# One core of Trainium2: the experts' last product with tokens on the output's partitions, and a new slot table

## What is computed

```python
h = _L0_tok_ref(x, ...)          # three layer norms and 5-wide convolutions, a fourth norm, res @ out_w + out_b: (64, 128, 64)
h = h + _L0_attn_ref(_layernorm(h), ...)   # 8 heads, logits -sum_w |q[s,h,w] - k[t,h,w]| / 8, softmax, values twice (a and a transposed)
h = h + _L0_ffn_ref(_layernorm(h), ...)

# _L0_ffn_ref: 32 experts, one per token
logits = xf @ router_w.T + router_b
idx = jnp.argmax(logits, axis=-1)
h = relu(einsum('nd,ndh->nh', xf, W1[idx]) + b1[idx])      # hidden size 16
out = relu(einsum('nh,nhd->nd', h, W2[idx]) + b2[idx])
```

## Time and profile before

| | us |
|---|---|
| median of 3 runs | 3468.23 (3464.18 to 3468.46) |
| the profiled execution | 3481.97 |
| its span, first to last instruction | 3480.2 |
| VectorE busy | 3130.7 (90%) |
| TensorE matmuls busy | 3227.9 (93%) |
| GpSimd busy | 2849.9 (82%) |
| ScalarE busy | 2577.4 (74%) |

### The profile page before, as it was taken

One profiled execution on the slowest core, in us unless ns is written; L12 is line 12 of the kernel. 1 busy time (PEld: TensorE's weight loads), 2 busy tenths in 40 slices (PEclk: granted clock), 3 DMA queues, 4 the chain that ended last, 5 costly groups with the idle time before them and its releaser, 6 DMA issues. The chain is left out here.

```text
span 3480.2 us, 78005 instructions
## 1 busy us (share of the span) xinstructions
PE 3227.9 (93%) x23116; PEld 2461.7 (71%) x23116; DVE 3130.7 (90%) x4358; ACT 2577.4 (74%) x4378; POOL 2849.9 (82%) x2728
## 2 busy tenths in 40 slices
PE   8899999999999999999999999999999999999888
PEld 6677777776777777777777777767777777777655
DVE  5899999999999999999999999999999999999876
ACT  3777787777777777777777777777777777777763
POOL 3788888888888888888888888888888888888874
PEclk9999999999999999999999999999999999999988
DMA  6778777778777778777777777787777787777773
GB/s 136 152 156 161 154 158 158 153 154 166 155 152 158 153 153 166 156 156 153 156 157 158 157 157 154 154 165 153 157 158 153 155 163 157 155 155 153 157 152 70
DMA packets 199652, 534.96 MB, mean 154 GB/s; under 512 B 69142, under 2 KB 133398, under 8 KB 150968
## 3 DMA queue, kind: packets, MB, share of 16 engines
q0 software_dynamic: 73728, 492.86, 71.4%
q1 hardware_dynamic: 125880, 41.54, 5.9%
HBM read 10.93 MB, written 2.10 MB: 4 GB/s over the span
## 5 line engine op out<-in xcount | busy, mean ns | idle before, releaser
L925 DVE TENSOR_REDUCE S<-psU 128x16 f32<-128x1024 f32 x2216 | 2629.9, 1217 | 235.4 <-PE psU L487 220.9
L487 PE MATMUL psU<-flat,kT 99*128 99x256 bf16 x16384 | 2291.6, 275 | 189.9 <-DVE S L925 119.4
L712 ACT ACTIVATE absd<-psU 128x1024 f32<-128x1024 f32 x1880 | 1913.4, 1023 | 587.0 <-PE psU L487 575.9
L487 PEld LDWEIGHTS psU<-flat,kT 99*128 99x128 bf16 x16384 | 1498.0, 98 | 832.1 <-DVE S L925 316.8
L1183 POOL TENSOR_TENSOR absd<-absd 128x1024 f32<-128x1024 f32 (+2 forms) x512 | 1183.5, 2312 | 111.3 <-DMA absd<-absd 110.1
L1189 POOL TENSOR_TENSOR absd<-absd 128x512 f32<-128x512 f32 (+4 forms) x768 | 767.5, 999 | 60.2
L1171 POOL DMA_DIRECT2D absd<-absd x512 | 454.0, 887 | 244.8 <-ACT absd L712 186.2
L499 PE MATMUL psC<-c1in,w 128*128 128x384 f32 (+1 forms) x930 | 314.3, 421 | 17.0 <-DVE c1in L969 16.9
L591 PE MATMUL psZ<-P,v 128*128 128x256 f32 x1024 | 279.1, 379 | 0.0
L936 DVE TENSOR_REDUCE S<-absd 128x64 f32<-128x512 f32 (+4 forms) x512 | 264.3, 516 | 1.3 <-POOL absd L1189 1.3
L518 PE MATMUL psC<-c3in,w 128*128 128x128 f32 x1240 | 245.8, 282 | 1.7 <-DVE c3in L969 1.7
(11 more groups left out here) (180 smaller groups left out, 2266.8 us busy)
## 6 DMA issues: line engine op xcount, KB each, us to landing
absd<-absd POOLq DMA_DIRECT2D x379, 1024.0 KB, 8.1
absd<-absd POOLq DMA_DIRECT2D x98, 768.0 KB, 6.5
flat<-qparts SPq DMA_DIRECT2D x3072, 8.0 KB, 4.0
absd<-absd POOLq DMA_DIRECT2D x35, 512.0 KB, 4.6
xin<-in_x SPq DMA_DIRECT2D x32, 192.0 KB, 6.4
flat<-pattern SPq DMA_DIRECT2D x4, 768.0 KB, 10.9
out_h<-result SPq DMA_DIRECT2D x32, 64.0 KB, 6.1
w<-in_w SPq DMA_DIRECT2D x1, 1280.0 KB
```

Source lines behind the costliest of these rows:

```text
L487: mm = nc.tensor.matmul(psU[:, slot % PLACES, m], kT[0:ROWS + 3, b, m, :], flat[0:ROWS + 3, half % HALVES, :, lo:lo + BLOCK], start=True, ...
L712: nc.scalar.activation(absd[:, c % GROUPS, :, u], psU[:, slot % PLACES].rearrange("p (n a) s w -> p n (a s w)", n=2), ACT.Abs).then_inc(a_ ...
L925: nc.vector.tensor_reduce(S[:, b, hd, SB * c:SB * c + SB], psU[:, slot % PLACES].rearrange("p a s w -> p s a w"), AX.XY, ALU.add, apply_ab ...
```

## The change

The output product swaps its operands: hT (for the bias: the one-hot ohT) becomes the stationary block, one sample's 128 tokens at a time, and the weights with 64 columns the moving one. The result then has the tokens on its partitions, as h2 has. So there are ten matmuls of 64 columns instead of five of 256, the relus into fT and the transpose back go, and VectorE takes relu and addition in one `scalar_tensor_tensor`. The weights are held and loaded once. In the tables turnb goes from slot 45 to 48, route from 74 to 75, out is spread over 7 slots instead of 4, stat goes from 1 to 5, and the lists for the lead-in, the last pair and the idle matmuls are new. VectorE's result stays in slot 101.

```diff
--- before
+++ after
@@ -62,7 +62,7 @@
-SHARED_LAST = {8: (0, 2, 4, 6), 9: (0, 2), 10: (0, 1), 11: (0, 2), 12: (0, 3, 6), 13: (2, 4, 6), 14: (0, 2, 4), 15: (0, 3)}
+SHARED_LAST = {8: (0, 2), 9: (1, 3), 10: (0, 4), 11: (2, 6), 12: (0, 4), 13: (1, 5), 14: (0, 2, 4), 15: (0, 3)}
@@ -109,10 +109,10 @@
-EX_PE = Steps("fan turn route turnoh hida hidb out back")
+EX_PE = Steps("fan turn route turnoh hida hidb out")
 EX_DVE = Steps("h2 stat0 stat1 wait aggr0 aggr1 max rev0 rev1 max2 noh result")
 EX_POOL = Steps("var rstd mean shift")
-EX_ACT = Steps("x0 x1 turned0 turned noh oh relua relub relu0 relu")
+EX_ACT = Steps("x0 x1 turned0 turned noh oh relua relub")
@@ -126,23 +126,23 @@
-AT1 = dict(vf=3, vb=5, v_len=0, turn_len=0, exp=25, exp_len=4, rden=38, scale=33, scale_len=19, turna=43, turnb=45,
+AT1 = dict(vf=3, vb=5, v_len=0, turn_len=0, exp=25, exp_len=4, rden=38, scale=33, scale_len=19, turna=43, turnb=48,
            pv=51, pv_len=3, half=52, sum=54, tanh=55, gate=60)
 AT_AT = (AT0, AT1)
 SECOND = 66
-EX_AT = dict(fan=62, h2=62, rstd=61, x=65, turn=67, route=74, pick=76, turnoh=82, hida=87, hidb=89, hid_len=0, out=92,
-             out_len=4, back=100)
-NORM_AT = dict(stat=1, rstd=2, x=9, turn=24, part1=20, rest1=19, part2=50, part3=50, hx=82)
+EX_AT = dict(fan=62, h2=62, rstd=61, x=65, turn=67, route=75, pick=76, turnoh=82, hida=87, hidb=89, hid_len=0, out=92,
+             out_len=7, result=101)
+NORM_AT = dict(stat=5, rstd=2, x=9, turn=24, part1=20, rest1=19, part2=50, part3=50, hx=82)
 HAND_AT = dict(xT=12, hx=83)
 TOK_AT = dict(copy=3, a=7, conv1=14, len1=22, b=47, conv2=56, len2=10, c=67, conv3=76, len3=33, d=112, turn=121,
               out=126, root=0, gap=4)
-LEAD_IN = [(36, 18), (41, 21), (52, 22), (56, 24), (59, 24), (66, 29), (71, 37), (77, 37), (79, 39), (81, 41),
-           (81, 56), (117, 68), (118, 75), (128, 78)]
-LEAD_LAST = (92, 111, 124)
-LEAD_TAIL = 0
-WEIGH = (2, 3)
+LEAD_IN = [(21, 11), (40, 16), (42, 16), (44, 24), (54, 24), (54, 24), (66, 27), (66, 27), (66, 28), (66, 28),
+           (75, 54), (117, 68), (128, 82)]
+LEAD_LAST = (90, 111, 117)
+LEAD_TAIL = 4
+WEIGH = (4, 5)
@@ -181,7 +181,7 @@
-STILL = dict(turna=18, fan=0, turn=21, route=9, turnoh=13, hida=7)
+STILL = dict(turna=20, fan=2, turn=26, route=4, turnoh=8, hida=6)
@@ -239,8 +239,8 @@
-        we2 = sb("we2", [T, 4, 2, LAT])
-        be2 = sb("be2", [T, 2, LAT])
+        we2 = sb("we2", [T, 4, LAT])
+        be2 = sb("be2", [T, LAT])
@@ -299,7 +299,6 @@
-        fT = sb("fT", [T, T])
@@ -347,12 +346,12 @@
-            (w3[:], a["w3"]), (b3[:], a["b3"]), (ln1g_col[:], a["ln1g_col"]), (ln1b_col[:], a["ln1b_col"]), (wout[:], a["wout"]),
-            (bout[:], a["bout"]), (rank[:], a["rank"]), (we2[:, :, 0, :], a["we2"]), (we2[:, :, 1, :], a["we2"]),
+            (w3, a["w3"]), (b3, a["b3"]), (ln1g_col, a["ln1g_col"]), (ln1b_col, a["ln1b_col"]), (wout, a["wout"]),
+            (bout, a["bout"]), (rank, a["rank"]), (we2, a["we2"]),
         ]
         parts_of = [
             (wqv[0:65, :], a["wqv"]), (wfan[0:65, :], a["wfan"]), (wroute[0:65, :], a["wroute"]),
-            (we1[0:65, :], a["we1"]), (we1[96:128, :], a["shut"]), (be2[0:E, 0, :], a["be2"]), (be2[0:E, 1, :], a["be2"]),
+            (we1[0:65, :], a["we1"]), (we1[96:128, :], a["shut"]), (be2[0:E, :], a["be2"]),
@@ -403,7 +402,7 @@
-                    sp.dma_start(dst, src).then_inc(loaded, 16)
+                    sp.dma_start(dst[:], src).then_inc(loaded, 16)
@@ -628,19 +627,17 @@
-                for q in spread(slot, EX_AT["out"], EX_AT["out_len"], 5):
-                    if q == 0:
-                        take_bank(ex_act, EX_ACT.after(p, "relu"))
-                    if q == 2 and other is not None:
+                for n in spread(slot, EX_AT["out"], EX_AT["out_len"], 10):
+                    b, q = n // 5, n % 5
+                    if n == 0:
+                        take_bank(ex_dve, EX_DVE.after(p, "result"))
+                    if n == 2 and other is not None:
                         pe.wait_ge(ex_act, EX_ACT.after(p, "relub"))
-                    mm = nc.tensor.matmul(psZ[:, 0:256], (be2[:, :, :] if q == 4 else we2[:, q, :, :]).rearrange("p a w -> p (a w)"),
-                                          ohT[:, :] if q == 4 else hT[:, q, :], start=(q == 0), stop=(q == 4))
-                    if q == 4:
+                    mm = nc.tensor.matmul(psZ[:, b * LAT:b * LAT + LAT],
+                                          ohT[:, b * T:b * T + T] if q == 4 else hT[:, q, b * T:b * T + T],
+                                          be2[:, :] if q == 4 else we2[:, q, :], start=(q == 0), stop=(q == 4))
+                    if n == 9:
                         mm.then_inc(ex_pe, 1)
-                if slot == EX_AT["back"]:
-
-                    take_bank(ex_dve, EX_DVE.after(p, "result"))
-                    nc.tensor.transpose(psZ[:, 0:2 * LAT], fT[:, :], ident[:, :]).then_inc(ex_pe, 1)
@@ -868,11 +865,6 @@
-                if slot == EX_AT["out"] + EX_AT["out_len"]:
-                    act.wait_ge(ex_pe, EX_PE.after(p, "out"))
-                    for b in range(2):
-                        nc.scalar.activation(fT[b * LAT:b * LAT + LAT, :], psZ[b * LAT:b * LAT + LAT, b * T:b * T + T],
-                                             ACT.Relu).then_inc(ex_act, 1)
@@ -1057,11 +1049,11 @@
-                if slot == EX_AT["back"] + 1:
-                    dve.wait_ge(ex_pe, EX_PE.after(p, "back"))
+                if slot == EX_AT["result"]:
+                    dve.wait_ge(ex_pe, EX_PE.after(p, "out"))
                     if not (isinstance(p, int) and p == 0):
                         dve.wait_ge(stored, 16 * p)
-                    nc.vector.tensor_tensor(result[:, :, :], zl, h2[:, :, :], ALU.add).then_inc(ex_dve, 1)
+                    nc.vector.scalar_tensor_tensor(result[:, :, :], zl, 0.0, h2[:, :, :], ALU.max, ALU.add).then_inc(ex_dve, 1)
@@ -1116,8 +1108,8 @@
-                        nc.vector.memset(be2[32:64, :, :], 0.0).then_inc(ones, 1)
-                        nc.vector.memset(be2[64:128, :, :], 0.0).then_inc(ones, 1)
+                        nc.vector.memset(be2[32:64, :], 0.0).then_inc(ones, 1)
+                        nc.vector.memset(be2[64:128, :], 0.0).then_inc(ones, 1)
                         for t in (x1T, x1T_late):
                             nc.vector.memset(t[64:65, :], 1.0).then_inc(ones, 1)
                         nc.vector.memset(gT[64:65, :, :], 2.0).then_inc(ones, 1)
```

## The result

The changed kernel takes 3479.85 us, the median of 20 runs (3471.79 to 3490.97), against 3468.39 us for 20 runs of the kernel before (3463.84 to 3479.25): ratio 1.0028, 95% interval 1.0019 to 1.0036. It is slower by about 10 us, where 4.9 us less was forecast, and it lies 1.9 us above the range of 3446 to 3478.

A forecast was written before the change was run, and what follows sets the result against it. VectorE taken as most loaded, only its waits for TensorE units winnable. Steady pairs -2.8, lead-in -1.5, last pair +0.3, tail -0.9 sum to -4.9 us, from 3468.23 to 3463.3 us; range 3446 to 3478.

The forecast's parts named there:

- The output product: Slots 92 to 98: VectorE's waits shrink, but ScalarE closes the stretch and gives the gain back; -0.06 us a pair.
- turnb: Slot 45 to 48: transposes go where TensorE waits for ScalarE; -0.03 us a pair, +0.1 if the copy comes late.
- stat: Norm's statistics, slot 1 to 5: GpSimd held no longer than now, 0; +0.3 us if they came 1 us late.
- What bounds the kernel: VectorE is most loaded; only its idle time waiting for TensorE units, 7 us a pair, can be won.
- Rival (2): Slots 97 and 98: two late matmuls delay unit 98 and VectorE waits; +14.6 us, 3478 us; chance 0.14.
- Rival (1): Output product's stretch: ScalarE isn't its end and the hole is really won; 15.5 us, 3448 us; chance 0.22.
- Rival (3): TensorE's waits for flat: transfers move by half, 17 us, to 3446 or 3480 us; chance 0.08 faster, 0.03 slower.
- Rival (4): Slots do nothing and only the kernel's ends act: 3466 us; chance 0.53 together with the main forecast.
- The passes: Output product on TensorE: twenty passes of 64 moving columns at 0.105 us each, 2.1 us against 2.2 before.
- Lead-in: Start of the kernel: unit 0 starts near 55.2 us; -1.5 us, from -3 to 0.
- Last pair and tail: SHARED_LAST gives VectorE four more units, +0.3 us (-2 to +3); chain after the last product loses relu and transpose, -0.9.
- The base: Whole kernel: profiled execution lies 13.7 us above the runs' median 3468.23; the same 4.9 us is taken from that median.

The follow-up runs named there:

- c4: Kernel before with the swapped product, turnb at 48, route at 75 and out over 7 slots, all else as before: 3474.13 us, ratio 1.0014.
- b2: Changed kernel with turnb, route, out, stat and all lists as before, so the swapped product alone: 3467.79 us, ratio 0.9997 to before.
- c1: Kernel before with one number changed, stat in slot 5 instead of 1: 3477.41 us, ratio 1.0018.
- c3: Changed kernel with stat back in slot 1 and LEAD_TAIL 1 instead of 4: 3474.17 us, ratio 1.0009 to before.
- d3: b2 with the new idle matmul counts and the first sample's eight exponentials laid over slots 93 to 95, out over 4 slots: 3471.30 us, ratio 1.0009 to before.
- d4: d3 with out spread over 7 slots instead of 4: 3455.03 us, ratio 0.9964 to before.
- c2: c1 with the changed kernel's lead-in lists: 3471.49 us, ratio 1.0010 to before.
- b4: Changed kernel with SHARED_LAST, the list for the last pair, as before: 3475.20 us, ratio 1.0026 to before.

## Why the prediction was wrong

**Sum.** Forecast -4.9 us, measured +10 us (0.0028 x 3468). By parts, as ratios give them: the swap with the old slots -1 (0.9997, uncertain by 3); turnb and out +4.3 by the traces, +6 by c4 against b2; stat +6 to +6.6 (each ratio uncertain by 4 to 5); lead-in, last pair and idle matmuls nothing that can be told. -1 + 4.3 + 6.3 = +9.6; with such uncertainties, that it meets the measured 10 so closely is in part luck.

**What bounds the kernel: right, but incomplete.** The sum was judged by VectorE's waits alone. TensorE's own idle time was taken as harmless wherever VectorE lies behind. It isn't: moving it, with VectorE's work unchanged, cost 6 us in c1, and the granted clock fell with it.

**stat, the step that failed most.** GpSimd "holds its next group's DMA and tree, but not longer than now: 0". What was asked there, whether GpSimd comes late, was answered rightly: slots 0 to 16 keep their median of 13.97 us. The mechanism that costs 6 us, the granted clock, was not among the rivals at all. The trace of before had shown it: its clock falls to half for 3.4 us at 389 and at 1761 us, both in slots 12 to 16 of a pair, and a middle stretch with a clock of 1.00 doesn't say that all pairs are like it. That such stretches come more often with stat in slot 5 is shown by c1 and c3. That it is the bunching of TensorE's idle time that brings them is argued from c1 and d3, which bunched it for different reasons; which property of it counts was not measured, and single pairs of before (at 389 and 1761 us) fall with the same waits as their neighbours. The Trainium skill describes such a thing in "TensorE: Matmul & The Clock Gate", section "A second HAM failure mode: psum-queue depth-cycling": short idle times between groups of matmuls that cycle through PSUM make the clock swing between its levels and cost throughput. By that page, which the prediction cited for the weight loads only, this would have been a rival; the runs agree with it in kind, and give it a price here of 0.18% and 0.19% of the time (c1, and c3 against after).

**turnb, the second step that failed.** The waits moved as forecast, and the copy ended as forecast: at 1154.8 in before's time (1156.43 less the 1.64 us by which slot 42 of this pair begins later). What was wrong is that this is "just when pv wants it, behind the unit that is complete at 1155.07". pv doesn't stand behind the end of that unit's row: in the trace of before its first weight load begins at 1154.80 and its first matmul at 1154.91. With units 50 and 51 now 0.08 us earlier, the load could have begun near 1154.7; it begins 0.11 us behind the copy's end, after a wait of 0.19 us. -0.03 was taken; the bound "if the copy comes late, +0.1" is what was measured, and the choice between them was worth 4 us in 31 pairs.

**The output product, right in mechanism, short in size.** VectorE's waits ahead of 91 to 95 fell to 1.30 us (forecast 1.2), TensorE waits for ScalarE ahead of unit 97, and unit 98 comes no earlier. Forecast -0.06 us a pair, measured +0.04 (-0.08 to slot 99, +0.12 behind it; c4 against b2). The reciprocal did go earlier, but unit 98 was complete at 1198.22 in before's time instead of 1198.15, and VectorE, which now waits for it, takes 1.23 us for this reduction, where it took 1.18 directly behind the reciprocal. Rival (2) named this place, and at 1198.22 the kernel came within 0.04 us of its point of decision, 1198.26; its full price of 0.47 us a pair was far too high. Rival (1) did not occur in after, and d4 shows that it was ScalarE that prevented it. Rival (3) did not occur either: the waits for flat are 31.8 us in 33 cases, as before. Rival (4), that only the ends act, 3466 us, is near b2 with 3467.79, whose slots are the old ones.

**The passes.** Six passes of 64 columns take 0.62 us from start to start in b2, 0.103 each, where 0.105 was taken. By the load rule of the Trainium skill ("TensorE: Matmul & The Clock Gate", section "LDWEIGHTS (loading the stationary operand)") it would be an estimated 107 ns for 128 columns, and the trace stands within 4% of it.

**Lead-in.** Unit 0 was forecast near 55.2 us and came at 54.7 (55.5 in c2), so that step worked. -1.5 us was booked for it, and it isn't there at the end of pair 0; c2 can't tell its share from nothing.

**Last pair and tail.** +0.3 was taken for SHARED_LAST; b4 gives 0.0002 between the kernels, no effect that can be measured. From VectorE's last reduction of psU on, nine kernels with the new product take 30.2 to 30.4 us and after 29.4, and the four with the old one 31.0, 31.0, 32.6 and 32.6: the product saves 0.6 us or more there, in agreement with -0.9, and the scatter of 1.6 us allows no closer word. In the two chains it is 0.57 us, where -0.98 + 0.25 - 0.1 = -0.83 was forecast for the same part: the wait and the twenty passes cost 0.41 us more than the ten passes did, not 0.15.

**The base.** 13.7 us between the profiled execution and the median were carried over as a constant. They weren't one: they were for the most part half-clock time at the two ends, and they also put the rows for the last pair in an untypical state.

## What to carry to other kernels

A step moved on an engine can cost time though that engine does the same work, when it moves TensorE's idle time and the granted clock falls more often: look at the granted clock pair by pair, not at the mean of a stretch, and compare the kernels' mean clocks over many runs. When one engine's wait is shortened ahead of a second engine that ends the stretch, neither edit shows alone; the two have to be made together, as d4 shows beside c4 and d3. Where a moved copy lands within 0.1 us of its reader, take the late side, and compare its end with the reader's first weight load, not with the end of the row ahead. Take a second profile before trusting the first one's ends.

## What was new about the hardware

The granted clock of a kernel whose TensorE is busy for 93% of the span falls to half for 3.4 us at a time in the middle of the run, at one place of the loop, and each such stretch costs some 1.4 to 1.5 us (15.45 against 13.98 in c1's pairs; 15.39 against 13.97 in the first profile of before). It happened in 0 to 17 of 27 pairs, by the slots chosen. Within one kernel, too, the timed runs follow it: after's 20 runs go from 3471.8 us at a clock of 0.994 to 3485.2, the mean of the three at 0.986.

A float32 pass with 128 stationary columns and a new stationary block each time takes 0.103 us with 64 moving columns (six in 0.62 us, b2) and 0.22 with 256 (pv in before, six in 1.30 us), so quartering the moving columns only halves it. And a copy that a matmul reads as stationary block has to be there ahead of the matmul's own turn: in before the first weight load of pv begins 0.11 us ahead of its first matmul, and in after it begins 0.11 us behind the end of the copy that it waits for.

VectorE's reduction of 1024 values takes 1.225 us after a wait and 1.216 without one (medians of after's trace), 0.01 us of difference. Directly behind some short instructions it is shorter, the most at unit 98 behind the reciprocal, with 1.17 to 1.18 us.
